# First attention of a two-layer network: the value sums turned by VectorE in 32x32 blocks, with the queries stored in another order

## The chip, the cores and the metric

The kernel runs on one core of a Trainium2 chip, as one program. The metric is the device time of one execution in microseconds (us). Before the change three runs took 5074.21, 5076.88 and 5078.27 us; the median is 5076.88 us.

## The reference

The input is x, 4 batches of 2048 tokens of 256 features, float32. Four blocks follow, each with a layer norm before it, a layer norm after it and a residual sum: a bidirectional scan with decay, a routed mixture with 32 experts, an attention with 16 heads of 16 features and rotary positions, and a sliced attention with 8 heads. The change is in the third:

```python
xq = (x @ wq.T).reshape(B, S, N_HEAD, HEAD_DIM)      # N_HEAD 16, HEAD_DIM 16
xk = (x @ wk.T).reshape(B, S, N_HEAD, HEAD_DIM)
xv = (x @ wv.T).reshape(B, S, N_HEAD, HEAD_DIM)
q = _apply_rope(xq, cos, sin)
k = _apply_rope(xk, cos, sin)
scores = jnp.einsum('bqhd,bkhd->bhqk', q, k) / jnp.sqrt(HEAD_DIM)
attn = jax.nn.softmax(scores, axis=-1)
out = jnp.einsum('bhqk,bkhd->bqhd', attn, xv)
```

B is 4 and S 2048, so there are 64 pairs of batch and head; below each of them is called a head.

## The kernel before

The program is a row of phases, one after the other, with a barrier between them: norm, scan, gate, experts, rope, attention (`at1`), sliced projections, second attention (`at2`), final. Every phase writes each engine's instructions by hand, in order; engines meet only at semaphores. An engine runs its instructions in the order in which they are written, so an instruction that waits holds all behind it.

*The phase before the attention* (`phase_rope`, tag r4) goes through 16 groups of 512 tokens. For each it projects queries, keys and values, turns the pairs, transposes queries and keys to features by tokens (PE into PQ), copies them with ACT into QF (`take_qk`, k = 0 and 1 queries, 2 and 3 keys), and splits them on GpSimd into a rounded part HI and a rest LO, which together hold full float32 for matmuls in the faster float32r. SP stores them with `store_qkv`, two groups behind the projections: the values (`VB`, 1 MB), then HI and LO of the queries (a = 0), then HI and LO of the keys (a = 1). Before its next use VB, HI and LO wait for the semaphore `l_st` of the stores of two groups ago; ACT's `values` is the first to do so. After this on the same queue come the loads of a later group.

*The attention* (`phase_attention` with `TWO` true) makes for each head 64 score tiles of 128 keys by 512 queries, one in each step t of a window of 64 steps. Three things run at once:

- The row maxima, which softmax needs before the exponentials, are computed one head ahead from a second product of queries and keys: PE writes tiles MX (128 queries by 1024 keys, two matmuls) into a ring of two (`RING`), DVE reduces each to a column of NM4 (`maxima`). There are 32 such tiles in a head, one at each even step. At step 50 PE turns the maxima of the next head, ACT copies them (NMF), and GpSimd and SP bring them into two more rows of QT, so that the score matmul subtracts them itself.
- The scores: PE multiplies KT by QT into one of three PSUM slots S (`NSR`), ACT takes the exponential into PB. The score of step t waits for the exponential of step t-3.
- The values: PE multiplies PB by VS, in blocks of 128 keys, each over four steps' tiles, and adds them up in one PSUM buffer AV. VS is 32 columns wide: 16 features, then a column of ones, which gives the softmax's divisor, then zeros. Four chunks of 512 queries stand in AV one below the other, 32 partitions each. A block kb is done in two halves of 256 queries (`PARTS`), the first at step `value_step(kb)` = 4 kb + 6 and the second two steps later. The steps past 63 fall into the next window: block 15 at its steps 2 and 4, and block 0 of the next head at step 6.

*The end of a head*, which the change is about, stands in the next window. At step 4 ACT copies AV into AVS (`put_values`); PE's first AV matmul of the next head waits for that copy. At step 7 (`OUT_STEP`) PE turns AVS with four 128x128 transposes into a slot S (`turn_values`), and ACT copies the slot into FO (`take_values`). At step 11 DVE takes the reciprocals of the divisors, GpSimd multiplies (`normalise_turned`), and SP stores. The transposes take a place in the ring of S, which is why a window has `SITEMS` = 66 places.

```python
PARTS = 2 if TWO else 1
WP = W // PARTS
END_STEP = value_step(NBLK - 1) + 2 * (PARTS - 1)
OUT_STEP = END_STEP + 3 - NSB
```

## Time and profile before

| what | us |
|---|---|
| median of three runs | 5076.88 |
| the profiled execution, its own time | 5076.77 |
| its span, first to last record | 5074.3 |
| PE busy in the span | 4656.5 (92%) |
| DVE busy | 4191.1 (83%) |
| ACT busy | 3425.1 (67%) |
| GpSimd busy | 1333.4 (26%) |

The profile is of one execution, and all shares in it are averages over nine phases with different limits. So a phase is looked at by its stretch of time, given in us from the start of the span. A row of a timeline has the start in us, the length in us, the engine, the line of the kernel, the operation, what it writes and what it reads with the tile's shape (partitions times elements; PE gives rows of the array times columns), how many like it stand in a row, and in brackets how long the engine was idle before and what ended that. Idle time under some 0.1 us is not listed. Two instructions of one engine overlap a little: the next starts before the last has fully ended. PE counts a float32 matmul as two records. PEld is the load of weights, which runs beside PE. A row of stretches has the bounds, the length, the busy time and number of instructions of PE, PEld, DVE, ACT and POOL (GpSimd), then the clock granted to PE (1.00 is 2.4 GHz), the busy share of the DMA engines and what they moved in GB/s.

### The profile page before, as it was taken

What the parts mean: (1) busy time and instruction counts of PE and PEld (TensorE: products, weight loads), DVE (VectorE), ACT (ScalarE), POOL (GpSimd) and SP (SyncE); (2) the same over time, 40 slices, a digit from 0 to 9 for tenths busy, and PEclk for the clock granted to TensorE, in tenths of its full rate; (3) what the DMA queues carried; (4) which work ended last, traced back from release to release, by engine and by line L of the source; (5) the groups of instructions that cost most, each with busy time, mean ns of one, the idle gap of its engine ahead of it and who ended that gap; (6) DMA issues with size and microseconds to landing.
All of it is one profiled execution on the core that took longest, in us unless ns stands there. A gap on an engine that the chain in (4) does not pass through costs nothing. (4 is left out here: it accounts for less than half of the span.)

```text
span 5074.3 us, 90035 instructions
## 1 busy us (share of the span) xinstructions
PE 4656.5 (92%) x33915; PEld 2063.8 (41%) x33915; DVE 4191.1 (83%) x5487; ACT 3425.1 (67%) x6144; POOL 1333.4 (26%) x881
## 2 busy tenths in 40 slices
PE   6998776896999999999999999999998889999993
PEld 3333542562333333333333333333334445555532
DVE  6999640796999999999999999999993877777736
ACT  4878110232888888888888888888885426666663
POOL 2333210462000000000000000000001229999992
PEclk9999887995999999999999999999997769999996
DMA  5111569686333333333333333333313831322305
GB/s 183 58 54 42 187 241 390 201 271 136 49 49 49 49 49 52 53 53 53 49 49 49 49 49 49 54 54 54 49 20 125 297 101 43 82 61 73 79 5 169
DMA packets 383090, 479.51 MB, mean 94 GB/s; under 512 B 164544, under 2 KB 277984, under 8 KB 365760
## 3 DMA queue, kind: packets, MB, share of 16 engines
q1 hardware_dynamic: 369376, 455.41, 38.5%
q10 hardware_dynamic: 13280, 18.35, 1.1%
q8 instruction: 267, 4.37, 0.4%
q14 instruction: 167, 1.37, 0.1%
HBM read 315.71 MB, written 155.58 MB: 93 GB/s over the span
## 5 line engine op out<-in xcount | busy, mean ns | idle before, releaser
L792 DVE TENSOR_REDUCE at_NM<-at_MX 128x1 f32<-128x1024 f32 (+1 forms) x3008 | 3085.7, 1050 | 300.5 <-PE at_MX L614 272.2
L734 ACT ACTIVATE at_PB<-at_S 128x512 f32<-128x512 f32 x5056 | 2720.4, 597 | 587.6 <-PE at_S L643 465.6
L614 PE MATMUL at_MX<-at_KT,at_QT 48*128 48x512 f32 (+1 forms) x5056 | 1920.6, 455 | 58.6 <-DMA at_VS<-v 43.9
L643 PE MATMUL at_S<-at_QT,at_KT 50*128 50x512 f32 (+1 forms) x5056 | 1900.0, 441 | 6.1 <-ACT at_PB L734 5.8
L655 PE MATMUL at_AV<-at_PB,at_VS 128*32 128x256 f32 (+1 forms) x18304 | 1568.6, 414 | 16.6 <-ACT at_AVS L742 15.6
L643 PEld LDWEIGHTS at_S<-at_QT,at_KT 50*128 50x128 f32 (+1 forms) x5056 | 801.6, 187 | 879.0 <-ACT at_PB L734 773.6
L614 PEld LDWEIGHTS at_MX<-at_KT,at_QT 48*128 48x128 f32 (+1 forms) x5056 | 791.2, 190 | 310.2 <-DVE at_NM L792 215.6
L655 PEld LDWEIGHTS at_AV<-at_PB,at_VS 128*32 128x32 f32 x18304 | 363.3, 108 | 859.8 <-ACT at_PB L734 747.5
L548 POOL CAST at_NMR<-at_NMF 16x128 fp32r<-16x128 f32 x79 | 22.1, 279 | 1626.6 <-ACT at_NMF L747 1626.6
L575 POOL TENSOR_TENSOR at_SUM<-at_SUM,at_PB 128x2048 f32<-128x2048 f32 x90 | 415.1, 4612 | 10.9
L935 PE MATMUL wkv_PQ<-wkv_XT,wkv_WT 128*128 128x512 f32 x768 | 341.3, 601 | 50.5 <-DVE wkv_DL L1058 34.1
L575 POOL TENSOR_TENSOR at_SUM<-at_PB 128x2048 f32<-128x2048 f32 x75 | 352.3, 4701 | 30.8 <-ACT at_PB L734 30.1
L558 POOL TENSOR_TENSOR at_O<-at_FO,at_REC 128x256 f32<-128x256 f32 x64 | 39.8, 622 | 1007.4 <-DVE at_REC L803 1007.4
L935 PEld LDWEIGHTS wkv_PQ<-wkv_XT,wkv_WT 128*128 128x128 f32 x768 | 144.9, 192 | 246.3 <-issue 195.0
L1013 POOL TENSOR_TENSOR wkv_EV<-wkv_E2S,wkv_V 128x1024 f32<-128x1024 f32 x32 | 75.5, 2360 | 312.0 <-DVE wkv_MN L1035 132.6
L1223 PE MATMUL r_PA<-r_OC,r_A 128*128 128x256 f32 x512 | 114.8, 383 | 12.5 <-DMA r_A<-ycat 12.5
L1824 PE MATMUL r_QK<-r_WC,r_XT 128*128 128x512 f32 x256 | 120.2, 593 | 0.5 <-DVE r_WC L1983 0.5
L2152 ACT ACTIVATE rows<-moe_PH 128x1024 f32<-128x1024 f32 x8 | 8.2, 1024 | 162.9 <-PE moe_TP L2194 132.1
L1510 PE MATMUL r_PO<-r_XT,r_WS 128*128 128x512 f32 (+2 forms) x136 | 94.9, 861 | 17.8 <-ACT r_XT L1539 17.8
L1223 PEld LDWEIGHTS r_PA<-r_OC,r_A 128*128 128x128 f32 x512 | 97.3, 193 | 27.0 <-DVE r_OC L1331 14.0
L747 ACT ACTIVATE at_NMF<-at_S 16x128 f32<-16x128 f32 x79 | 21.1, 267 | 118.0 <-PE at_S L634 118.0
L2129 DVE COPY rows<-moe_TP 128x128 f32<-128x128 f32 x8 | 2.3, 293 | 115.2 <-PE moe_TP L2194 115.2
(213 smaller groups left out, 3492.6 us busy)
## 6 DMA issues: line engine op xcount, KB each, us to landing
at_QT<-qk SPq DMA_DIRECT2D x402, 128.0 KB, 4.9
moe_W<-in_w SPq DMA_DIRECT2D x48, 1024.0 KB, 11.8
at_KT<-qk SPq DMA_DIRECT2D x384, 128.0 KB, 6.6
qk<-r_HI SPq DMA_DIRECT2D x52, 512.0 KB, 4.7
qk<-r_LO SPq DMA_DIRECT2D x52, 512.0 KB, 5.3
at_VS<-v SPq DMA_DIRECT2D x96, 256.0 KB, 8.7
at_KT<-qk SPq DMA_DIRECT2D x96, 256.0 KB, 6.1
ycat<-wkv_Y SPq DMA_DIRECT2D x32, 512.0 KB, 2.6
```

Of the source, the lines that this page charges most:

```text
L558: nc.gpsimd.tensor_tensor(out, fo[:, :, :, 0:DH], REC[s % 2][:, :, :].to_broadcast([P, W // P, NCH, DH]), ALU.mult).then_inc(norm_done, 1)
L575: nc.gpsimd.tensor_tensor(total[:, :, :], other, PB[:, k:k + NCH, :], ALU.add).then_inc(sum_done, 1)
L614: ins = nc.tensor.matmul(MX[r][:, a, :], q_of(s)[h:h + NQ, b * P:(b + 1) * P], k_of(it, s, b * P // W)[h:h + NQ, (c + a) * W:(c + a + 1) * W],
L643: nc.tensor.matmul(SP_[item(it, s, "score", t)[1]][:, :], k_of(it, s, c)[h:h + NQ + 2, kb * P:(kb + 1) * P], q_of(s)[h:h + NQ + 2, c * W:( ...
L655: ins = nc.tensor.matmul(AV[c * VW:(c + 1) * VW, cols], v_of(it, s, c)[:, kb, :], PB[:, (NCH * kb + c) % NPB, cols], start=first, stop=last)
L734: nc.scalar.activation(PB[:, t % NPB, :], SP_[r][:, :], ACT.Exp, scale=scale).then_inc(exp_done, 1)
L792: nc.vector.tensor_reduce(NM4[:, b, c:c + 1], MX[r][:, :, :].rearrange("p a n -> p (a n)"), AX_X, ALU.max, negate=True).then_inc(ring_got, 1)
L935: ins = nc.tensor.matmul(PQ[q][:, tt * 512:(tt + 1) * 512], WT[:, cc, row:row + P], XT[b % 2][:, cc, t0:t0 + 512], start=(cc == 0), stop=( ...
L1013: nc.gpsimd.tensor_tensor(EV[s][:, :], E2S[s][:, :], V[s][:, :], ALU.mult).then_inc(pv, 1)
L1223: ins = nc.tensor.matmul(PA[u][:, j, :], A[u][:, q, j * P:(j + 1) * P], OC[:, q, :], start=(q == 0), stop=(q == NC - 1))
L1510: ins = nc.tensor.matmul(PO[a][:, h, :], WS[0:k, c, lo:lo + P], XT[u][0:k, c, :], start=(c == 0), stop=(c == len(ks) - 1))
L1824: ins = nc.tensor.matmul(QK[j % 2][:, :], XT[u][:, c, j * P:(j + 1) * P], WC[:, c, 0:2 * D], start=(c == 0), stop=(c == CC - 1))
```

## The change

It has three parts.

1. *The turn.* The copy AVS, the four transposes by PE and the copy FO by ACT are gone for this attention. DVE has one `transpose` of 128x512 from AV in PSUM to FO in SBUF; it turns each block of 32x32 in its place. The block of chunk c and columns 32 j to 32 j + 31 then has 32 queries on partitions 32 c to 32 c + 31 and the 32 columns of the values side by side. It stands at step 2 of the next window, the reciprocal at step 4, the multiply on GpSimd at step 6. The semaphore `avs_ready`, for which PE's next block 0 waits, now comes from DVE.
2. *The last value block.* Both halves of block 15 are done in one step (`part_step`), so that AV is complete at step 2. A window has 65 places in the ring of S.
3. *The order of the queries.* For each partition to hold the queries of its own rows of the output, query 128 b + 32 c + q is now column 512 c + 32 b + q of QT. ACT's copy `take_qk` writes the queries in that order, in runs of 32, and each of HI and LO of the queries is stored with two transfers of 128 partitions by four runs of 128 elements (512 B) in place of one with runs of 512 elements (2 KB). Keys and values are stored as before.

```diff
-    SITEMS = NSB + 1 + TWO
+    SITEMS = NSB + 1
...
-    END_STEP = value_step(NBLK - 1) + 2 * (PARTS - 1)
-    OUT_STEP = END_STEP + 3 - NSB
+    END_STEP = value_step(NBLK - 1)
+
+    def part_step(kb, part):
+
+        return value_step(kb) + (2 * part if kb < NBLK - 1 else 0)
...
             def normalise_turned(it, s):
-                fo = FO[s % 2][:, :].rearrange("p (j c d) -> p j c d", j=W // P, c=NCH)
-                out = O[s % 2][:, :, :].rearrange("p (c j) d -> p j c d", c=NCH)
                 wait(pool, ostored[s % 2], 8 * NSTORE * it - 8 * NSTORE * (s % 2), pool_step)
                 wait(pool, rec_done, it + 1, pool_step)
-                nc.gpsimd.tensor_tensor(out, fo[:, :, :, 0:DH],
-                                        REC[s % 2][:, :, :].to_broadcast([P, W // P, NCH, DH]),
+                nc.gpsimd.tensor_tensor(O[s % 2][:, :, :], FO[s % 2][:, :, 0:DH],
+                                        REC[s % 2][:, :].to_broadcast([P, W // VW, DH]),
                                         ALU.mult).then_inc(norm_done, 1)
...
-            def turn_values(it, s, r):
-
-                wait(pe, avs_ready, it + 1, pe_step)
-                for j in range(W // P):
-                    ins = nc.tensor.transpose(SP_[r][:, j * P:(j + 1) * P], AVS[s % 2][:, j * P:(j + 1) * P],
-                                              ident[:, :])
-                ins.then_inc(s_put, 1)
-
...
-                        if value_step(kb) + 2 * part == t:
+                        if part_step(kb, part) == t:
                             values(n, s, kb, part)
...
-            def take_values(it, s, i, r):
-                wait(act, norm_done, it - 1)
-                wait(act, s_put, i + 1)
-                nc.scalar.activation(FO[s % 2][:, :], SP_[r][:, :], ACT.Copy).then_inc(fo_got, 1)
...
+            def turn_values(it, s):
+
+                wait(dve, norm_done, it - 1)
+                wait(dve, av_done, NBLK * (it + 1))
+                nc.vector.transpose(FO[s % 2][:, :, :].rearrange("p j d -> p (j d)"), AV[:, :]).then_inc(avs_ready, 1)
+
             def invert_turned(it, s):
-                fo = FO[s % 2][:, :].rearrange("p (j c d) -> p j c d", j=W // P, c=NCH)
-                wait(dve, norm_done, it - 1)
-                wait(dve, fo_got, it + 1)
-                nc.vector.reciprocal(REC[s % 2][:, :, :], fo[:, :, :, DH]).then_inc(rec_done, 1)
+                wait(dve, avs_ready, it + 1)
+                nc.vector.reciprocal(REC[s % 2][:, :], FO[s % 2][:, :, DH]).then_inc(rec_done, 1)
...
                         out = qk[a, part].rearrange("(c p) t -> p c t", p=P)
+                        if a == 0:
+                            for c in range(CC):
+                                sp.dma_start(out[:, c, :].rearrange("p (s t) -> p s t", s=E4)[:, :, e * P:(e + 1) * P],
+                                             tile[u][:, c, :].rearrange("p (s t) -> p s t", s=E4).bitcast(F32)).then_inc(l_st[u], 16)
+                            continue
                         sp.dma_start(out[:, :, e * GT:(e + 1) * GT],
                                      tile[u][:, 2 * a:2 * a + 2, :].bitcast(F32)).then_inc(l_st[u], 16)
...
-                nc.scalar.activation(QF[k % 2][:, :], PQ[:, :], ACT.Copy).then_inc(qk_got, 1)
+                out, in_ = QF[k % 2][:, :], PQ[:, :]
+                if k < CC:
+                    out = out.rearrange("p (c j q) -> p j c q", c=E4, j=J)
+                    in_ = in_.rearrange("p (j c q) -> p j c q", c=E4, j=J)
+                nc.scalar.activation(out, in_, ACT.Copy).then_inc(qk_got, 1)
```

How it moves the instructions. First PE at the end of the first head, in the second window, before; each row has the line, the operation, what it writes and reads, and how often. S are scores, MX the tiles of maxima, AV the sums of values.

```order
L614 MATMUL at_MX<-at_KT,at_QT 128x512 x2
L643 MATMUL at_S<-at_QT,at_KT 128x512
L655 MATMUL at_AV<-at_PB,at_VS 32x256 x4
L643 MATMUL at_S<-at_QT,at_KT 128x512
L614 MATMUL at_MX<-at_KT,at_QT 128x512 x2
L643 MATMUL at_S<-at_QT,at_KT 128x512
L655 MATMUL at_AV<-at_PB,at_VS 32x256 x4
L674 MATMUL at_S<-at_ident,at_AVS 128x128 x4
L643 MATMUL at_S<-at_QT,at_KT 128x512
L614 MATMUL at_MX<-at_KT,at_QT 128x512 x2
L643 MATMUL at_S<-at_QT,at_KT 128x512
```

and with the change:

```order
L638 MATMUL at_S<-at_QT,at_KT 128x512
L650 MATMUL at_AV<-at_PB,at_VS 32x256 x8
L638 MATMUL at_S<-at_QT,at_KT 128x512
L611 MATMUL at_MX<-at_KT,at_QT 128x512 x2
L638 MATMUL at_S<-at_QT,at_KT 128x512 x2
L611 MATMUL at_MX<-at_KT,at_QT 128x512 x2
L638 MATMUL at_S<-at_QT,at_KT 128x512
L650 MATMUL at_AV<-at_PB,at_VS 32x256 x4
```

The four transposes between the last AV of one head and the next scores are gone; the four AV matmuls of the last half have joined the four before them (x8), and the two scores after the next MX pair stand with no AV between them.

Next DVE, over the same window, from the end of the maxima's preparation on, before (L792 are the tiles of maxima, L797 the last step of a head's maxima):

```order
L797 TENSOR_REDUCE at_NM<-at_NM 128x16
L792 TENSOR_REDUCE at_NM<-at_MX 128x1 x17
L803 RECIPROCAL at_REC<-at_FO 128x16
L792 TENSOR_REDUCE at_NM<-at_MX 128x1 x15
L797 TENSOR_REDUCE at_NM<-at_NM 128x16
```

and with the change:

```order
L768 TENSOR_REDUCE at_NM<-at_NM 128x16
L763 TENSOR_REDUCE at_NM<-at_MX 128x1 x13
L774 STREAM_TRANSPOSE at_FO<-at_AV 128x512
L763 TENSOR_REDUCE at_NM<-at_MX 128x1
L778 RECIPROCAL at_REC<-at_FO 128x16
L763 TENSOR_REDUCE at_NM<-at_MX 128x1 x18
L768 TENSOR_REDUCE at_NM<-at_NM 128x16
```

The transpose stands one tile of maxima before the reciprocal, and the reciprocal three tiles earlier than before.

Last SP in the phase before the attention, the stores of one group and the loads behind them, before:

```order
L1709 DMA x<-r_X 128x1024
L1716 DMA v<-r_VB 128x16x128
L1722 DMA qk<-r_HI 128x2x512
L1722 DMA qk<-r_LO 128x2x512
L1722 DMA qk<-r_HI 128x2x512
L1722 DMA qk<-r_LO 128x2x512
L1701 DMA r_A<-routed 32x512
```

and with the change:

```order
L1687 DMA x<-r_X 128x1024
L1694 DMA v<-r_VB 128x16x128
L1702 DMA qk<-r_HI 512x1x128 x2
L1702 DMA qk<-r_LO 512x1x128 x2
L1705 DMA qk<-r_HI 128x2x512
L1705 DMA qk<-r_LO 128x2x512
L1679 DMA r_A<-routed 32x512
```

HI and LO of the queries are two transfers each (x2), of 512 runs of 128 elements; nothing else moves.

## Rows read from the trace of the kernel before

**Rows 1.** Stretches: the phase before the attention, and the attention.

```profile
903.70:1172.00 268.30, 249.47 (x1032) 162.17 (x1032) 223.94 (x532) 79.15 (x160) 161.99 (x198) 0.96 0.78 259
1172.00:3862.00 2690.00, 2637.75 (x24896) 995.51 (x24896) 2513.05 (x2180) 2293.08 (x4289) 93.39 (x196) 0.98 0.36 49
```

**Rows 2.** The same view, of 2500 us in the middle of the attention.

```profile
1290.00:3790.00 2500.00, 2484.85 (x23819) 938.12 (x23819) 2400.27 (x2083) 2193.86 (x4104) 82.78 (x184) 1.00 0.36 50
```

**Rows 3.** Timeline of DVE over one head of the attention.

```profile
1419.92 0.24 DVE L803 RECIPROCAL at_REC<-at_FO 128x16 f32<-128x16 f32 x1
1420.09 18.54 DVE L792 TENSOR_REDUCE at_NM<-at_MX 128x1 f32<-128x1024 f32 x15
1438.66 0.19 DVE L797 TENSOR_REDUCE at_NM<-at_NM 128x16 f32<-128x32 f32 x1
...
1458.36 2.45 DVE L792 TENSOR_REDUCE at_NM<-at_MX 128x1 f32<-128x1024 f32 x2 [0.90 <-PE at_MX L614]
1460.72 0.25 DVE L803 RECIPROCAL at_REC<-at_FO 128x16 f32<-128x16 f32 x1
```

**Rows 4.** Timeline of PE at the end of the same head.

```profile
1413.76 0.40 PE L643 MATMUL at_S<-at_QT,at_KT 50*128 50x512 f32 x1
...
1414.09 0.64 PE L655 MATMUL at_AV<-at_PB,at_VS 128*32 128x256 f32 x8
...
1414.66 0.50 PE L643 MATMUL at_S<-at_QT,at_KT 50*128 50x512 f32 x1
...
1415.00 0.40 PE L643 MATMUL at_S<-at_QT,at_KT 50*128 50x512 f32 x1
...
1415.64 0.64 PE L655 MATMUL at_AV<-at_PB,at_VS 128*32 128x256 f32 x8 [0.24 <-ACT at_AVS L742]
...
1416.21 0.66 PE L674 MATMUL at_S<-at_ident,at_AVS 128*128 128x128 f32 x4
...
1416.79 0.49 PE L643 MATMUL at_S<-at_QT,at_KT 50*128 50x512 f32 x1
```

**Rows 5.** Timelines: DVE ahead of the first scores, ACT and PE in the last head.

```profile
1227.37 17.06 DVE L792 TENSOR_REDUCE at_NM<-at_MX 128x1 f32<-128x1024 f32 x15 [1.36 <-PE at_MX L614]
...
3845.09 11.80 ACT L734 ACTIVATE at_PB<-at_S 128x512 f32<-128x512 f32 x21
...
3856.95 1.07 PE L655 MATMUL at_AV<-at_PB,at_VS 128*32 128x256 f32 x16 [0.18 <-ACT at_PB L734]
```

**Rows 6.** Groups of DVE instructions by line: busy us, mean ns of one.

```profile
L1066 DVE TENSOR_TENSOR_SCAN wkv_DEN<-wkv_E1S,wkv_DEN,wkv_E2S 128x1024 f32<-128x1024 f32 x32 | 77.2, 2411 | 0.0
...
L809 DVE TENSOR_TENSOR at_O<-at_L,at_AVS 128x512 f32<-128x512 f32 x15 | 10.2, 682 | 78.9 <-ACT at_L L760 78.9
```

**Rows 7.** Phase before the attention: two stretches, then timelines of ACT and PE.

```profile
1008.00:1010.00 2.00, 2.00 (x15) 1.65 (x13) 1.93 (x4) 0.82 (x3) 1.92 (x3) 1.00 1.05 290
1012.00:1014.00 2.00, 2.00 (x8) 1.07 (x8) 1.77 (x8) 0.60 (x1) 0.28 (x2) 1.00 1.04 383
...
1003.65 0.84 ACT L1898 ACTIVATE r_VB<-r_PV,r_RS 128x256 f32<-128x256 f32 x2 [3.74 <-DMA qk<-r_LO]
...
1018.16 0.84 ACT L1898 ACTIVATE r_VB<-r_PV,r_RS 128x256 f32<-128x256 f32 x2 [2.85 <-PE r_PV L1834]
...
1005.03 0.66 PE L1844 MATMUL r_PQ<-r_ident,r_QR 128*128 128x128 f32 x4
...
1020.11 0.60 PE L1844 MATMUL r_PQ<-r_ident,r_QR 128*128 128x128 f32 x4
```

**Rows 8.** What ended ACT's idle time before L1898: us in all, times.

```profile
  PE r_PV L1834: 85.6, 28
  DMA qk<-r_LO: 13.8, 4
```

**Rows 9.** Timeline at the end of the attention, ACT's copy and DVE's reciprocal.

```profile
3858.08 0.60 ACT L742 ACTIVATE at_AVS<-at_AV 128x512 f32<-128x512 f32 x1 [1.19 <-PE at_AV L655]
...
3860.25 0.25 DVE L803 RECIPROCAL at_REC<-at_FO 128x16 f32<-128x16 f32 x1 [34.81 <-ACT at_FO L752]
```

More of the change, by code:

```diff
@@ L336, in places @@
         for t in range(NSB):
-            if TWO and t == OUT_STEP and (not isinstance(n, int) or n > 0):
-                out.append(("out", 0))
             out.append(("score", t))
@@ L347, in item @@
         if not isinstance(n, int):
-            return SITEMS * n - TWO + 1 + k, (SITEMS * s - TWO + 1 + k) % NSR
-        i = SITEMS * n - (TWO if n else 0) + 1 + k
+            return SITEMS * n + 1 + k, (SITEMS * s + 1 + k) % NSR
+        i = SITEMS * n + 1 + k
         return i, i % NSR
@@ L368, in phase_attention @@
         PB = m.sb("PB", [P, NPB, W])
-        AVS = [m.sb(f"AVS{u}", [P, W]) for u in range(2)]
         NM4 = m.sb("NM4", [P, NBLK, NMX // NBLK])
@@ L376, in phase_attention @@
             O = [m.sb(f"O{u}", [P, NBLK, DH]) for u in range(2)]
-            REC = [m.sb(f"REC{u}", [P, W // P, NCH]) for u in range(2)]
-            FO = [m.sb(f"FO{u}", [P, W]) for u in range(2)]
+            REC = [m.sb(f"REC{u}", [P, W // VW]) for u in range(2)]
+            FO = [m.sb(f"FO{u}", [P, W // VW, VW]) for u in range(2)]
         else:
+            AVS = [m.sb(f"AVS{u}", [P, W]) for u in range(2)]
             ONES = m.sb("ONES", [P, VW])
@@ L588, in window @@
                         adds(*unit)
-                    if TWO and t == OUT_STEP + 4 and (not isinstance(n, int) or n > 0):
+                    if TWO and t == END_STEP + 4 - NSB and (not isinstance(n, int) or n > 0):
                         normalise_turned(n - 1, s + NBUF - 1)
@@ L626, in slot_free @@
                     wait(pe, exp_done, NSB * of + x + 1, pe_step)
-                elif kind == "turn":
+                else:
                     wait(pe, nmf_got, of + 2, pe_step)
-                else:
-                    wait(pe, fo_got, of, pe_step)
             def max_turn(it, r):
@@ L697, in window @@
                     tile = tile_at(t)
-                    if TWO and t == OUT_STEP and (not isinstance(n, int) or n > 0):
-                        slot_free(n, "out")
-                        turn_values(n - 1, s + NBUF - 1, item(n, s, "out")[1])
                     if tile and later(n, tile[0]):
@@ L737, in put_values @@
             def put_values(it, s):
-                if not TWO:
-                    wait(act, norm_done, it - 1)
+                wait(act, norm_done, it - 1)
                 wait(act, av_done, NBLK * (it + 1))
@@ L763, in window @@
                 for t in range(NSB):
-                    if TWO and t == OUT_STEP and (not isinstance(n, int) or n > 0):
-                        take_values(n - 1, s + NBUF - 1, *item(n, s, "out"))
                     exps(n, s, t)
                     for it, s_, t_ in running(n, s, t):
-                        if END_STEP == t_:
+                        if not TWO and END_STEP == t_:
                             put_values(it, s_)
@@ L777, in _ @@
             rounds(act, window)
-            put_values(N - 1, N - 1)
-            if TWO:
-                take_values(N - 1, N - 1, TAIL, TAIL % NSR)
-            else:
+            if not TWO:
+                put_values(N - 1, N - 1)
                 put_sums(N - 1)
@@ L830, in window @@
                             outputs(*unit)
-                    if TWO and t == OUT_STEP + 4 and (not isinstance(n, int) or n > 0):
+                    if TWO and t == END_STEP - NSB and (not isinstance(n, int) or n > 0):
+                        turn_values(n - 1, s + NBUF - 1)
+                    if TWO and t == END_STEP + 2 - NSB and (not isinstance(n, int) or n > 0):
                         invert_turned(n - 1, s + NBUF - 1)
@@ L834, in _ @@
             if TWO:
+                turn_values(N - 1, N - 1)
                 invert_turned(N - 1, N - 1)
@@ L1741, in _ @@
             for u in range(2):
[L1742 removed]
+                sp.wait_ge(l_st[u], 56 * NGR)
         @block.gpsimd
@@ L1773, in split @@
                 if k == 0:
-                    wait(pool, l_st[u], 80 * (g // 2))
+                    wait(pool, l_st[u], 112 * (g // 2))
                 wait(pool, qk_got, 4 * g + k + 1)
@@ L1894, in values @@
                 wait(act, rs1, g + 1)
-                wait(act, l_st[u], 80 * (g // 2))
+                wait(act, l_st[u], 112 * (g // 2))
                 for jj in range(2):
```

8 lines of the change are left out of this document (1 added, 7 removed).

## The prediction

> **What bounds the kernel now.** I read the profile from the outside in. The table of stretches first: the first attention takes 2690 us of the span, the stage before it (the one that writes its queries) 268 us [rows 1]. The change touches only these two. In 2500 us of the attention's middle PE is busy 2484.9 us, or 99.4%, DVE 96%, ACT 88%, at a granted clock of 1.00 [rows 2]. That PE is busy is not yet that it binds, so the next view is DVE's row of work in time: each head of 64 steps repeats after 1460.72 - 1419.92 = 40.80 us [rows 3]. Fifteen tiles of maxima take 18.57 us there (1420.09 to 1438.66), 1.238 us each, in which PE does a pair of steps. Where PE had nothing else to do, DVE took fifteen in 17.06 us, 1.137 each; where DVE had nothing to do, ACT took 21 exps in 11.80 us, 1.124 for two [rows 5]. So DVE has 0.10 us to spare in each 1.24 and ACT 0.11, and **PE sets the pace**.
>
> Then PE's timeline over one head's end [rows 4]. A pair of scores, with an MX pair beside it, starts at 1414.66 and the next at 1416.79, 2.13 apart where 1.24 is usual: 0.89 us is lost. The reader sees both parts: the AV matmuls at 1415.64 waited for ACT's copy of AV (after the score before them they would have begun 0.33 later, as 1413.76 and 1414.09 show; that score began at 1415.00, so 0.31 is lost), and four transposes hold PE from 1416.21 to the next score at 1416.79, 0.58. Together 0.89. DVE's idle 0.90 before its tile of 1458.36 [rows 3] is the same loss seen from behind. The rest of the 40.80 is 32 x 1.238 = 39.6 and about 0.3 at the turn of the maxima, which stays.
>
> **The change, part by part.**
>
> *PE and ACT at a head's end.* Four transposes, the copy into AVS and the copy into FO go, and with them the wait of AV for AVS: 0.89 us of PE per head in 63 of 64 heads. ACT's two copies (0.60 each) were off the bound, they only caused the wait.
>
> *The last value block.* Its second half moves from two steps later into the same step. PE's order has eight AV matmuls in one place and none in the next. The profile counts each as two records: eight records hold PE 0.57 (1414.09 to 1414.66), sixteen last 1.07 against 0.64 [rows 4, 5], so the double block holds 1.00. Call its start 0. From the rows, the second score of a pair starts 0.34 after the first (1414.66, 1415.00) and what follows 0.33 later. So the next scores start at 1.00, 1.34 and 1.67, the one after at 2.01, and that one needs the slot whose exp comes from the score of 1.00: done 0.49 later [rows 4], exp of 0.56 [rows 5], and by my estimate 0.1 of signals, 2.15. PE stands 0.14 us there, and the AV block after it starts at 2.34 + 0.14 = 2.48, which is where two pairs of 1.24 would put it. So what the merged block saves (1.00 for twice 0.57) the wait takes back, and the sum is 0; ACT catches up with its 0.11 per pair.
>
> *DVE's transpose.* The trace before has no such instruction. Below it lies the cheapest row with 512 columns from PSUM, 0.68 us (the multiply of the second attention); above it the scan, 2.41 for 1024, so 1.21 for 512 [rows 6]. I take 0.70, since it reads each column once as the multiply does; DVE starts its next instruction 0.07 before the end of the last (the reciprocal lasts 0.24 from 1419.92, the next starts at 1420.09 [rows 3]), so it takes 0.63 of DVE. Where does it stand? Tile 2's matmuls end at 0.05, so DVE works on it until 1.2; the AV block ends at 1.07, so the transpose does not wait. It holds DVE until 1.8, tile 4 until 2.95 (done, and its slot free, at 3.05), the reciprocal adds 0.17 (1419.92 to 1420.09), tile 6 until 4.25 (free at 4.35). PE needs those two slots at 3.05 and 4.29. So DVE's extra work just about fits in the slack of the ring of two tiles; with a signal's 0.06 I allow 0.12 us for it per head. Queued behind the transpose on DVE is tile 4, and PE's tile 8 waits for that. PE's first AV matmul of the next head (at 2.48) waits for the transpose, done at 1.9: covered by 0.6.
>
> The Trainium skill (VectorE: DVE Perf Modes, The three transpose paths) gives 311 ns for 128x128 bf16 on DVE against 390 ns on TensorE. No run here shows it; four such blocks would make 1.24 us, an estimate from that page, and by that the head would gain 0.23 and the time be 5066 us, as in the first rival. Against it stand the reciprocal of 16 columns at 0.24 us [rows 3] and 512 columns at 0.68 [rows 6]: some 0.23 of any DVE instruction is fixed, and four times 0.31 would count that four times.
>
> *Gain per head:* 0.89 - 0.12 = 0.77, with the bounds 0.89 (nothing stands) and 0.26 (a transpose of 1.21 costs 0.51 more). 63 x 0.77 = 48.5 us.
>
> *The last head.* From the end of AV to the reciprocal: 3858.08 to 3860.25, 2.17 us [rows 9]. Now one transpose, 0.65: saves 1.5 us. GpSimd's multiply reads another layout of the same size and stays.
>
> *The stage before: queries stored in another order.* ACT copies with the same 512 columns, runs of 32: I take it as 0.60 still, and ACT is 70% idle there. The stores of HI and LO for the queries go from 2 transfers of 2 KB packets to 4 of 512 B, 32 more issues on SP, 2 in each of 16 groups. In front of them stands nothing new; behind them on SP are the key stores and the loads of a later group, which have a group's time in hand. In a stretch with 512 B packets (the values') the DMA engines move 290 GB/s, in one with 2 KB packets 383, both full [rows 7]. So 1.05 MB takes 3.62 us in place of 2.74: +0.88 us per group. The Trainium skill (DMA: Bandwidth & Descriptors, Specifications) has 512 B as the least size for line rate; the trace disagrees by that quarter, and its number decides (by the page the term would be 0). Is it hidden? A group takes 15.08 us (PE's transposes at 1005.03 and 1020.11), DMA is busy 78% on average [rows 1], so throughput is there. But ACT's scaling of the values waits for the landing of the stores of two groups ago: in 4 of 32 cases DMA released it [rows 8]. At 1003.65 it did [rows 7], 0.57 us after the place that the next group's (1018.16 - 15.08) gives. After it comes ACT's QF copy, 0.6 us as any of 512 columns, and PE waits for that: 1018.16 + 0.84 + 0.60 = 1019.6 against 1020.11, 0.5 us to spare, and none in the group before [rows 7]. So a landing 0.88 later passes on up to 0.88 to PE in a group like the first and little in others, and a late PE gives the next group's stores more time. I take 0.25 us x 14 groups = 3.5, and 0.9 for the last stores, after which the attention may begin: +4.4 us. Bounds: 0, and 14 x 0.88 + 1.8 = 14 us.
>
> **Sum.** Against the profiled execution's own 5076.77 us (span 5074.3, 2.5 around it; the median of the three runs is 5076.88, the same): -48.5 - 1.5 + 4.4 = -45.6, so 5031 us.
>
> **The rivals.**
> 1. *DVE becomes the bound.* The transpose costs what a scan costs, 1.21 us. DVE has little slack: 0.10 per tile. Tile 4 comes 0.51 later, PE stands for its slot, and the head gains 0.77 - 0.51 = 0.26. 63 x 0.26 = 16.4, the last head saves 1.0 and the stores cost 4.4: 5064 us. For it: DVE is at 96%. Against it: a scan carries each result into the next, a transpose does not; the multiply's 0.68 is the nearer row [rows 6].
> 2. *The query stores bind the stage before.* All of the 0.88 in every group and 1.8 at its end, +14 instead of +4.4: 5040 us. For it: the landing already is on the edge. Against: 28 of 32 waits end with PE.
> 3. *Slower: PE waits for the transpose.* AV has one buffer. If the 32x32 turn of 4-byte data takes 1.9 us, over half again the scan's pace, everything behind it on DVE comes 1.2 later than in my sum: the head loses 0.12 + 1.2 against 0.89 gained, +0.43 x 63 = 27, with the stores 5108 us. It decides from about 1.47 us of transpose on, where 0.77 is used up. For it: nothing of the kind is in the trace. Against it: even the scan is at 1.21.
> 4. *The change does nothing*, because what looks like PE's loss is a wait that comes back elsewhere (in ACT's exps): 5075 to 5082 us. Against it: ACT's pace alone is 1.12 [rows 5].
>
> **How the numbers follow.** Forecast 0.72, rival 1 0.11, rival 2 0.09, rival 3 0.05, rival 4 0.03. The predicted time is the forecast's 5031. Its own ends are 5019 (all 0.89 gained, 56.1, 1.5 for the last head, the stores free) and 5050 (0.50 per head, 31.5, with the 1.5, and the stores at 6); rival 2 lies inside. To leave out no more than 2 in 10, the range goes from 5019 to 5058, most of the way to rival 1. A change of under 0.2%, 10 us, cannot be told from none: faster 0.88 (rival 1, at 13 us, counts mostly here), the same 0.07, slower 0.05.
>
> **What would show it.** In the profile after: the row of the transpose, 0.65 to 0.75 us, 64 of them; the head's period from reciprocal to reciprocal 40.0 us; pairs of scores around the double AV block 1.67 and 0.67 apart and the pair after them at its usual place; DVE's idle time from MX at the head's end nearly gone, and PE waits for DVE's maxima that were not there before, about 0.1 us each; the stage before at 15.1 to 15.4 us per group with more of ACT's waits ended by LO's stores; the attention's stretch 2640 us. It is wrong if the period stays over 40.5 (rival 1 or 4: the transpose's duration tells which), or if the stage before grows by over 10 us.

## The result

The change takes 5029.51 us (median of 4 runs, 5026.30 to 5031.53), the kernel before on the same chip 5075.56 (4 runs). The ratio is 0.9904, 95% interval 0.9890 to 0.9918: faster by about 1%. Predicted was 5031, from 5019 to 5058. The profiled execution took 5029.49 us, its span 5027.3, 47.0 less than before.

| | before | after |
|---|---|---|
| span, us | 5074.3 | 5027.3 |
| PE busy | 4656.5 (92%) | 4622.3 (92%) |
| DVE busy | 4191.1 (83%) | 4207.0 (84%) |
| ACT busy | 3425.1 (67%) | 3361.4 (67%) |
| head's period, reciprocal to reciprocal, mean of 61 | 40.83 | 40.10 |
| first store of x to first load of KT | 261.01 | 265.79 |
| first load of KT to last reciprocal | 2681.54 | 2633.82 |

The last two lines are read from the timelines of SP's queue and of DVE: 915.23, 1181.02 and 3814.84 after, 917.70, 1178.71 and 3860.25 before. The attention gives 47.7 us, the stage before it takes 4.8, what lies behind the attention is 1.6 shorter and what lies ahead of both 2.5, though the change touches neither; together 47.0.

The groups of the page that answer to the change (the line, engine, operation, tiles, count, busy time, mean ns, idle time before and what ended it), in the changed kernel:

```profile
L763 DVE TENSOR_REDUCE at_NM<-at_MX 128x1 f32<-128x1024 f32 (+1 forms) x3008 | 3066.3, 1049 | 241.1 <-PE at_MX L611 216.2
...
L715 ACT ACTIVATE at_PB<-at_S 128x512 f32<-128x512 f32 x5056 | 2712.1, 597 | 628.3 <-PE at_S L638 503.7
...
L555 POOL TENSOR_TENSOR at_O<-at_FO,at_REC 128x256 f32<-128x256 f32 x64 | 39.9, 624 | 749.8 <-DVE at_REC L778 749.8
```

The stretches, as [rows 1, 2] before; the columns are the same:

```profile
903.70:1172.00 268.30, 251.65 (x1032) 161.90 (x1032) 223.60 (x532) 79.06 (x160) 158.96 (x195) 0.96 0.82 254
...
1290.00:3700.00 2410.00, 2407.83 (x23146) 917.88 (x23139) 2370.48 (x2104) 2093.57 (x3907) 81.00 (x180) 1.00 0.38 51
```

PE was busy 99.4% of the middle; now it is 99.9%. In the page's groups DVE's wait for MX is 216 us in the whole program, where it was 272. ACT waits for scores 504 us for 466 before, in which time it has fewer copies to make; it is off the path. GpSimd's multiply lasts 0.62 us as before.

DVE over one head, as [rows 3]:

```profile
1413.77 0.71 DVE L774 STREAM_TRANSPOSE at_FO<-at_AV 128x512 f32<-128x512 f32 x1
1414.40 1.19 DVE L763 TENSOR_REDUCE at_NM<-at_MX 128x1 f32<-128x1024 f32 x1
1415.51 0.23 DVE L778 RECIPROCAL at_REC<-at_FO 128x16 f32<-128x16 f32 x1
1415.67 21.93 DVE L763 TENSOR_REDUCE at_NM<-at_MX 128x1 f32<-128x1024 f32 x18
1437.64 0.19 DVE L768 TENSOR_REDUCE at_NM<-at_NM 128x16 f32<-128x32 f32 x1
1437.86 5.96 DVE L763 TENSOR_REDUCE at_NM<-at_MX 128x1 f32<-128x1024 f32 x5
1444.03 9.94 DVE L763 TENSOR_REDUCE at_NM<-at_MX 128x1 f32<-128x1024 f32 x8 [0.22 <-PE at_MX L611]
1453.89 0.71 DVE L774 STREAM_TRANSPOSE at_FO<-at_AV 128x512 f32<-128x512 f32 x1
...
1455.63 0.23 DVE L778 RECIPROCAL at_REC<-at_FO 128x16 f32<-128x16 f32 x1
```

The turn of the values lasts 0.71 us, in all 64 heads between 705 and 718 ns. The idle 0.90 of [rows 3] is gone; 0.22 at the turn of the maxima stays. PE's timeline at the same head's end, as [rows 4], and ACT's:

```profile
1411.86 0.50 PE L638 MATMUL at_S<-at_QT,at_KT 50*128 50x512 f32 x1
...
1412.53 1.07 PE L650 MATMUL at_AV<-at_PB,at_VS 128*32 128x256 f32 x16
1413.53 0.50 PE L638 MATMUL at_S<-at_QT,at_KT 50*128 50x512 f32 x1
...
1413.87 0.39 PE L638 MATMUL at_S<-at_QT,at_KT 50*128 50x512 f32 x1
...
1414.11 0.40 PE L638 MATMUL at_S<-at_QT,at_KT 50*128 50x512 f32 x1
...
1414.78 0.50 PE L638 MATMUL at_S<-at_QT,at_KT 50*128 50x512 f32 x1
1415.21 0.64 PE L650 MATMUL at_AV<-at_PB,at_VS 128*32 128x256 f32 x8
1415.78 0.50 PE L638 MATMUL at_S<-at_QT,at_KT 50*128 50x512 f32 x1
```

```profile
1414.13 2.06 ACT L715 ACTIVATE at_PB<-at_S 128x512 f32<-128x512 f32 x4 [0.59 <-PE at_S L638]
```

From the pair at 1411.86 to the pair at 1415.78 it is 3.92 us, where three pairs take 3.72: PE still loses 0.20 per head. It does so ahead of the score of 1414.78. That one needs the slot of the score of 1413.53, whose exp starts at 1414.13, 0.10 after the score's end, and is done some 0.56 later, at 1414.69. No row of PE names a tile of maxima as what it waits for: between 1300 and 3800 us the view of the MX matmuls lists no wait for DVE, where it lists 62 with the turn done twice (run 3). PE stands for ACT's exp, which runs 2 and 4 bear out.

### The profile page after: what moved, and what is told of

Same layout as the page of the kernel before. It is cut to its first block and busy times, and to the rows that moved or that the text cites. A ratio compares the mean times of both kernels' runs of the same rounds, so it can differ in the third digit from the quotient of the medians.

```text
span 5027.3 us, 89365 instructions
## 1 busy us (share of the span) xinstructions
PE 4622.3 (92%) x33659; PEld 2057.7 (41%) x33659; DVE 4207.0 (84%) x5551; ACT 3361.4 (67%) x6016; POOL 1333.6 (27%) x881
## 5 line engine op out<-in xcount | busy, mean ns | idle before, releaser
L1885 ACT ACTIVATE r_VB<-r_PV,r_RS 128x256 f32<-128x256 f32 x64 | 26.8, 470 | 108.4 <-PE r_PV L1817 65.7
```

## The experiments

Totals of one kernel scatter by up to 21 us between executions, on one chip too (ten of run 1 lie between 5061.70 and 5082.63). So what decides below is the period of a head and the stretches of the profile; the ratio stands beside them. A period below is the time between two reciprocals, given with both; the mean of 61 heads of the same profile differs from it by 0.02 us at most, except in run 6, where both are given.

**1. The last block not merged.** Its second half back at two steps later, the turn at step 4.

```diff
-    END_STEP = value_step(NBLK - 1)
+    END_STEP = value_step(NBLK - 1) + 2 * (PARTS - 1)
-        return value_step(kb) + (2 * part if kb < NBLK - 1 else 0)
+        return value_step(kb) + 2 * part
```

> The change with its second part undone: the second half of block 15 stands at step 4 again, DVE's transpose after tile 4, the reciprocal at step 6. Theory A: the merged block is what lets DVE turn ahead of tile 4. Without it the transpose starts when tile 4 is reduced, 2.47 us after the first half's start, and is done at 3.17, while PE wants AV for the next head at 2.48: PE waits 0.75 us per head in place of the 0.20 that the change still loses. 63 x 0.55 = +35: 5064 us, period of a head 40.65. Theory B: the 0.20 that is left comes from the merged block (the score after it is late, and an exp with it), and the transpose fits anywhere: -0.20 x 63 = -13: 5017 us, period 39.9.

Measured: period 1336.99 - 1296.31 = 40.68; 5069.87 us, ratio 0.9988 (0.9978 to 0.9998). PE at the head's end:

```profile
1334.94 0.40 PE L638 MATMUL at_S<-at_QT,at_KT 50*128 50x512 f32 x1
1336.01 0.64 PE L650 MATMUL at_AV<-at_PB,at_VS 128*32 128x256 f32 x8 [0.68 <-DVE at_FO L774]
```

The AV block would have started at 1335.27; it stands 0.74 until DVE's transpose is done. The transposes and ACT's copies are gone here too, and yet only 0.15 of the 0.89 is won. Merging the last block, which the prediction booked at 0, is what lets the turn run beside PE's work: it is worth 0.58 of the 0.73. The period came as theory A had it (40.65).

**2. A turn of 32 columns.** It leaves out 15 of 16 parts of the turn (the rest of FO holds ones), so that most of the attention's output is missing.

```diff
-                nc.vector.transpose(FO[s % 2][:, :, :].rearrange("p j d -> p (j d)"), AV[:, :])...
+                nc.vector.transpose(FO[s % 2][:, 0, :], AV[:, 0:VW])...
```

> The change with only 32 of the 512 columns of AV turned (the other columns of FO hold ones, so most of the attention's output is left out). DVE's instruction shrinks from 0.71 to about 0.2 us. Theory A: DVE's turn is hidden, the 0.20 us left per head are PE waiting for the exp behind the merged block: same time as the change, 5029 us within 3, period 40.1. Theory B: the 0.20 are the ring of two tiles, held by DVE: period 39.9, 5017 us.

Measured: period 1349.09 - 1308.97 = 40.12, 5031.05 us, ratio 0.9911 (0.9894 to 0.9928).

```profile
1307.30 0.20 DVE L774 STREAM_TRANSPOSE at_FO<-at_AV 128x32 f32<-128x32 f32 x1
1307.83 1.23 DVE L763 TENSOR_REDUCE at_NM<-at_MX 128x1 f32<-128x1024 f32 x1 [0.33 <-PE at_MX L611]
```

DVE gets 0.51 us back, waits 0.33 for PE before the next tile, and the period is the change's. So in the changed kernel the turn is free, and the 0.20 left is not DVE's.

**3. A second turn, elsewhere and in the same place.** Once in the middle of the window, where nothing depends on it:

```diff
+                    if TWO and t == 20 and n > 0:
+                        nc.vector.transpose(SCR[:, :], FO[(n - 1) % 2][:, :, :].rearrange("p j d -> p (j d)"))
```

> The change with one more transpose of 128x512 on DVE at step 20 of each window, from FO in SBUF to a tile that nobody reads. It adds 0.63 us of DVE per head at a place where DVE has nothing else to catch up with. Theory A (PE binds, DVE has 0.10 us of slack per tile and 0.5 us of lead in the ring): PE waits 0.05 to 0.15 us per head, 5032 to 5039 us. Theory B (DVE at 98% binds): all of it shows, 63 x 0.63 = 40: 5069 us.

and once right ahead of the turn that is there, from AV into a scratch tile:

```diff
+                nc.vector.transpose(SCR[:, :], AV[:, :])
```

> The change with the turn done twice at the same place, first into a tile that nobody reads, then into FO. 0.63 us more of DVE per head, as in the run with the transpose in mid-window (which cost 0.05 us per head), but ahead of tile 4. Theory A (after the merged block there is no lead left: tile 4 is reduced by 3.05 now and PE writes into its slot at 3.25): tile 4 is done at 3.7, PE waits 0.45 us for its slot, period 40.12 + 0.45 = 40.57, 63 x 0.45 = 28 more than the change: 5058 us. Theory B (the ring of two has 0.5 us of lead at every place): +0.05 again, 40.17, 5033 us.

Measured in the middle: period 1342.91 - 1302.75 = 40.16, 0.06 more than 40.10 (5038.18 us, ratio 0.9919, 0.9900 to 0.9937). At the head's end: 1342.97 - 1302.38 = 40.59, 0.49 more (5065.06 us, ratio 0.9973, 0.9957 to 0.9989). PE there, with the turn doubled:

```profile
1342.06 0.64 PE L651 MATMUL at_AV<-at_PB,at_VS 128*32 128x256 f32 x8
1342.63 0.50 PE L639 MATMUL at_S<-at_QT,at_KT 50*128 50x512 f32 x1
1343.10 0.50 PE L612 MATMUL at_MX<-at_KT,at_QT 48*128 48x512 f32 x2
```

and DVE:

```profile
1341.27 0.67 DVE L776 STREAM_TRANSPOSE at_FO<-at_AV 128x512 f32<-128x512 f32 x1
1341.86 1.19 DVE L764 TENSOR_REDUCE at_NM<-at_MX 128x1 f32<-128x1024 f32 x1
```

An MX pair starts with the score beside it, at 1342.63, elsewhere; here it is 0.47 later, because tile 4's maxima (1341.86, 1.19 long) end at 1343.05. DVE came to tile 4 0.59 later (1341.27 to 1341.86, the second turn less the overlap), so 0.10 of that is hidden and 0.49 is paid, through the ring's slot. That gives rival 3 its number: a turn of 0.71 + 0.10 + 0.73 = 1.54 us would use up the gain of a head, an estimate from these rows, where the prediction had 1.47.

**4. The score ahead of the double block.** Can the 0.20 be had? The score of step 3 goes ahead of the merged block, so that its exp is not the late one.

```diff
-                    scores(n, s, t)
+                    if not (TWO and t == 3 and n > 0):
+                        scores(n, s, t)
+                    if TWO and t == 2 and n > 0:
+                        scores(n, s, 3)
```

> The change with PE's score of step 3 placed ahead of the merged block of AV matmuls instead of behind it. ACT gets its exp in time, and the 0.2 us for which the score of step 6 waits for that exp should go. But AV is complete 0.33 us later, so DVE's transpose, tile 4 and its slot come about 0.2 to 0.3 us later. Theory A (the next wait, for tile 4's slot, takes its place at once): period 40.1, 5024 to 5032 us. Theory B (the exp is the only thing that stands): period 39.8 to 39.9, 5010 to 5016 us.

Measured: period 3738.79 - 3698.59 = 40.20, 0.10 worse; 5043.0 us, ratio 0.9926 (0.9907 to 0.9946). DVE and PE at another head's end:

```profile
1364.46 0.72 DVE L777 STREAM_TRANSPOSE at_FO<-at_AV 128x512 f32<-128x512 f32 x1
1365.10 1.19 DVE L766 TENSOR_REDUCE at_NM<-at_MX 128x1 f32<-128x1024 f32 x1
```

```profile
1365.94 0.50 PE L638 MATMUL at_S<-at_QT,at_KT 50*128 50x512 f32 x1
1366.34 0.51 PE L611 MATMUL at_MX<-at_KT,at_QT 48*128 48x512 f32 x2
```

The wait for the exp is gone. But the double block now stands behind one score more: DVE turns AV 2.13 after the start of the pair ahead of it (1362.33 in this trace), where in the change it was 1413.77 - 1411.86 = 1.91. Tile 4 is read until 1366.29, and the MX pair starts 0.40 after the score that it usually starts with. The next wait took the place of the one removed, and it is longer: theory A's mechanism, at 0.10 more than its 40.1. The run does not show what that wait would be with AV complete as early as in the change.

**5. The second half one step later.**

```diff
-        return value_step(kb) + (2 * part if kb < NBLK - 1 else 0)
+        return value_step(kb) + (2 * part if kb < NBLK - 1 else part)
```

> The change with the second half of block 15 one step later (step 3, behind that step's score) instead of in the same step. The score of step 3 is late by nothing, so no exp is late. AV is complete at 1.55 instead of 1.07 after the block's start. Theory A (two lanes bind at the end of a head, the exp's and the tile slot's): the transpose ends at 2.2, tile 4 at 3.4, PE wants its slot at 3.05 and waits 0.4 in place of the 0.2 for the exp: period 40.3, 5042 us. Theory B (only the late exp costs): period 39.9, 5017 us.

Measured: period 3723.12 - 3682.61 = 40.51, 0.41 worse; 5055.63 us, ratio 0.9956 (0.9942 to 0.9971). DVE:

```profile
1330.84 0.72 DVE L774 STREAM_TRANSPOSE at_FO<-at_AV 128x512 f32<-128x512 f32 x1 [0.37 <-PE at_AV L650]
```

Both expectations miss. DVE reaches the turn before AV is complete and stands 0.37, and tile 4 behind it (until 1331.48 + 1.18 = 1332.66) and PE's slot with it:

```profile
1332.41 0.50 PE L638 MATMUL at_S<-at_QT,at_KT 50*128 50x512 f32 x1
1332.72 0.51 PE L611 MATMUL at_MX<-at_KT,at_QT 48*128 48x512 f32 x2
```

That is theory A's wait; the head loses 0.21 more than A said (40.3), of which no run tells the parts. In the changed kernel DVE arrives just after AV is complete: 1413.77 against an end of 1412.53 + 1.07 = 1413.60. Three other orders of the head's end have now been tried (runs 1, 4 and 5), and the change's own is the best of them.

**6. The transposes alone.** The 0.89 of [rows 4] was split by reading into 0.58 for PE's transposes and 0.31 for ACT's copy. Here ACT copies AV to FO at step 4 as before, the last block is not merged, as in run 1, and DVE's turn is out: there is no turn by anyone, nor the division (the reciprocal reads ones). Of the edit, the copy and the reciprocal:

```diff
+                dst = FO[s % 2][:, :, :].rearrange("p j d -> p (j d)") if TWO else AVS[s % 2][:, :]
-                nc.scalar.activation(AVS[s % 2][:, :], AV[:, :], ACT.Copy).then_inc(avs_ready, 1)
+                nc.scalar.activation(dst, AV[:, :], ACT.Copy).then_inc(avs_ready, 1)
...
-                nc.vector.reciprocal(REC[s % 2][:, :], FO[s % 2][:, :, DH]).then_inc(rec_done, 1)
+                nc.vector.reciprocal(REC[s % 2][:, :], CST[:, :, DH]).then_inc(rec_done, 1)
```

> The change without DVE's turn: ScalarE copies the value sums from PSUM to FO at step 4, at the place where the kernel before copied them to AVS; no transposes by PE, no second copy, the second half of block 15 at step 4 as before. Left out: the turn of the values, and the division by the sums (the reciprocal reads a tile of ones). It splits the 0.89 us that PE lost per head before, 40.83 us per head, into the transposes and the wait for the copy. Theory A, the sum as predicted: the four transposes were lost in full, 0.58, and the wait for ScalarE's copy stays, 0.24 to 0.31, so a period of 40.2 to 40.3; PE's row of values of the next head still waits 0.2 to 0.3 for at_FO by ACT. Theory B: the place that the transposes took was partly cover for the copies and for DVE, so that taking them away gives less than 0.4: 40.45 or more. Theory C: with the transposes gone ScalarE's copy is no longer waited for either: 39.95 to 40.1, better than the change.

Measured: period 1342.50 - 1302.22 = 40.28 for the first, and 40.23 as the mean of 61, which goes against the 40.83 before; 5039.45 us, ratio 0.9922 (0.9904 to 0.9940).

```profile
1300.65 0.40 PE L639 MATMUL at_S<-at_QT,at_KT 50*128 50x512 f32 x1
1301.29 0.64 PE L651 MATMUL at_AV<-at_PB,at_VS 128*32 128x256 f32 x8 [0.24 <-ACT at_FO L724]
```

The transposes, with ACT's second copy, cost 40.83 - 40.23 = 0.60, and the wait stays, 1301.29 - 1300.98 = 0.31: the split was right, theory A.

**7. The stage before the attention.** Three kernels, and then the change and the last of the three once more. First the old order of the query stores, with ACT's copy plain again (the attention then reads its queries in the old order, and its rows come out in another):

```diff
-                        if a == 0:
-                            for c in range(CC):
-                                sp.dma_start(... [:, :, e * P:(e + 1) * P], ...)
-                            continue
...
-                out, in_ = QF[k % 2][:, :], PQ[:, :]
-                if k < CC:
-                    out = out.rearrange("p (c j q) -> p j c q", c=E4, j=J)
-                    in_ = in_.rearrange("p (j c q) -> p j c q", c=E4, j=J)
-                nc.scalar.activation(out, in_, ACT.Copy).then_inc(qk_got, 1)
+                nc.scalar.activation(QF[k % 2][:, :], PQ[:, :], ACT.Copy).then_inc(qk_got, 1)
```

> The change with its third part undone: ACT copies the queries in token order and they are stored in 2 KB runs (so the attention's rows come out in a wrong order). Theory A: 512 B packets cost the phase before the attention what its stretch grew by, 4.8 us (first store to the attention's first load, 261.0 to 265.8): 5025 us, that stretch 261. Theory B: the growth is scatter between executions: 5029 us and a stretch near 266 or anywhere between.

Then the new number of transfers with the old pieces of 2 KB (a group's queries in four transfers, where before there were two):

```diff
-                                sp.dma_start(out[:, c, :].rearrange("p (s t) -> p s t", s=E4)[:, :, e * P:(e + 1) * P],
-                                             tile[u][:, c, :].rearrange("p (s t) -> p s t", s=E4).bitcast(F32))...
+                                sp.dma_start(out[:, c, e * GT:(e + 1) * GT],
+                                             tile[u][:, c, :].bitcast(F32))...
```

> The change, with the query stores still cut into one transfer per plane of 128 rows, but each of them with the old addresses: 128 rows of 2 KB in a piece where the change has pieces of 512 bytes. ScalarE still permutes. The rows of the queries end up in the wrong order. It tells the size of the pieces from the number of the transfers. Theory A (the pieces of 512 bytes make the stores slow): the stretch from the first store of x to the first load of KT, 261.01 us before, 265.79 with the change and 260.54 with the old stores, comes back to 261.0, at most 262. Theory B (four transfers in place of one, issued and completed one after the other, make them late): it stays at 265 to 266. Period of a head in attention 40.1 by both.

Then the change with a semaphore of their own for the values' stores, so that ACT's scaling of the values waits for these alone and not for the later stores of HI and LO:

```diff
+        v_st = [m.sem(f"v_st{u}") for u in range(2)]
-                sp.dma_start(out[:, :, e * J:(e + 1) * J, :], VB[u][:, :, :, :]).then_inc(l_st[u], 16)
+                sp.dma_start(out[:, :, e * J:(e + 1) * J, :], VB[u][:, :, :, :]).then_inc(v_st[u], 16)
...
-                wait(act, l_st[u], 112 * (g // 2))
+                wait(act, v_st[u], 16 * (g // 2))
```

> The change with a semaphore of its own for the stores of the values, so that ACT's scaling waits for the values' store alone and not for the queries' and keys'. GpSimd's split still waits for those. Theory A (the new stores cost time through this wait, which ended 11 of ACT's waits before L1885 after the change and 4 before it): the stretch from the first store of x to the attention's first load falls from 265.8 to 261.5 to 262.5, only the last stores stay longer; 5026 us. Theory B (512 B packets make the DMA engines the bound of that phase): stretch 265 to 266, 5029 us.

And the change and this kernel again, on one chip:

> The change once more, unchanged, timed on the same chip as the run after it, since totals of other chips cannot be set against each other below 0.2%. Period of a head 40.10 and rope stretch 265.8 again, attention from the first load of KT to the last reciprocal 2633.8. If single profiles scatter by more than 1 us in the rope stretch, the price of the stores is less sure than the difference of two profiles makes it look.

> The values' own semaphore once more, beside the change on the same chip. Theory A (the stores' delay reaches the end only through ScalarE's wait for buffers, and nothing later takes it up): the rope stretch is 261 to 262 as before, attention 2634 to 2636, and the median is 4 us less than that of the change, some 0.08%. Theory B (what the rope phase gains is lost behind it): stretch 261 to 262, median within 1 us of the change's.

The stretch, cut by the stores of x, of which there is one per group (from the timeline of SP's queue, in us):

| kernel | 1st to 2nd | 2nd to 16th, 14 groups | 16th to first load of KT | sum | ACT's waits ended by DMA | median, ratio (interval) |
|---|---|---|---|---|---|---|
| before | 12.01 | 210.84 | 38.16 | 261.01 | 4, 13.8 us | |
| the change | 12.01 | 214.56 | 39.22 | 265.79 | 11, 42.6 | above |
| the change again | 12.00 | 214.65 | 39.15 | 265.80 | 11, 42.6 | 5031.87, 0.9905 (0.9889 to 0.9922) |
| runs 1 to 6 (same stage) | 12.0 or 13.5 | 211.64 to 215.01 | 39.15 to 39.22 | 262.82 to 267.66 | 11 to 14, 42.7 to 49.4 | |
| old stores | 12.00 | 210.39 | 38.15 | 260.54 | 5, 17.0 | 5026.01, 0.9900 (0.9885 to 0.9916) |
| four transfers of 2 KB pieces | 12.01 | 213.07 | 38.18 | 263.26 | 12, 43.6 | 5031.54, 0.9910 (0.9895 to 0.9925) |
| own semaphore | 12.01 | 210.00 | 39.27 | 261.28 | none | 5034.74, 0.9916 (0.9901 to 0.9931) |
| own semaphore again | 13.37 | 210.00 | 39.29 | 262.66 | none | 5029.43, 0.9902 (0.9887 to 0.9916) |

Three things are seen. The third column of the stretch is 38.15 to 38.18 in the three kernels with pieces of 2 KB and 39.15 to 39.29 in all those with pieces of 512 bytes: **the size of the pieces costs 1.0 us at the end**, whatever the number of transfers. The 14 groups take 210.00, 15.0 each, as soon as ACT no longer waits for the stores of HI and LO: **all the rest is that wait**. And the wait goes with the number of transfers: four of 2 KB pieces have as much of it as the change (12 times, 43.6 us), two of 2 KB pieces little (4 and 5 times), here with four and then with two (the view of r_VB on ACT, what ended its idle time):

```profile
  DMA qk<-r_LO: 43.6, 12
```

```profile
  DMA qk<-r_LO: 17.0, 5
```

From the issue of a group's first query store to the landing of its last store, the median of the 3rd to 14th group is 11.77 and 11.55 us with two transfers, 12.80 with four of 2 KB pieces and 12.84 in the change; in the 16th group it is 7.98, 7.98, 8.00 and 8.73. So in the middle it is the number that makes the stores late, and at the end the pieces. As a time, the middle of the four transfers is 2.2 to 2.7 us above the kernels with two. In the kernels whose stage is the change's it varies between 211.6 and 215.0, so the 213.07 lies inside, and no run shows that the pieces add anything there. The sum, 263.26, met neither expectation (261 to 262, 265 to 266), since each of the two causes has its own place.

The wait in the lines of ACT, in this stage; in the change, then with the semaphore of their own:

```profile
L1885 ACT ACTIVATE r_VB<-r_PV,r_RS 128x256 f32<-128x256 f32 x64 | 26.8, 470 | 108.4 <-PE r_PV L1817 65.7 <-DMA qk<-r_LO 42.6
```

```profile
L1887 ACT ACTIVATE r_VB<-r_PV,r_RS 128x256 f32<-128x256 f32 x64 | 26.8, 470 | 97.1 <-PE r_PV L1819 97.1
```

DMA ended 11 of these waits with the change, 4 before [rows 8], none with the own semaphore.

Is that kernel faster than the change? By the stretch by 3.1 to 4.5 us; the medians on one chip, 5029.43 and 5031.87, differ by 2.4 in the expected sense, where single runs of each spread over 12 and 14 us. The first time its median was 5034.74, where 5026 was expected. As a total it is unclear: neither theory of the last expectation (4 us, within 1 us) is shown. The attention of the change took 2640.53 us this time, where 2633.8 was expected; the last section shows why.

## Why the prediction held

*PE sets the pace.* It does: a second turn in the middle of a window costs 0.06 of 0.63, and a turn of 0.20 us gains nothing.

*0.89 lost per head, 0.31 and 0.58.* Shown by run 6: 0.31 and 0.60.

*The merged block, "the sum is 0".* The times within it came as worked out, scores at 1.00 and 1.34 after its start. The third came at 1.58 for 1.67, the one that waits at 2.25 for 2.15, since ACT's exp began 0.10 after the score ended and the prediction counted this 0.1 on one side only. The AV block behind it came at 2.68 for 2.48: after standing, the score took 0.43 to the next block where 0.33 is usual. So PE stands 0.20 longer than the merging saves. What this step missed is what the merging is for: without it (run 1) the turn ends in PE's way, and 0.58 of the gain goes.

*DVE's turn, 0.70, and 0.12 for the ring.* The turn is 0.71. The 0.12 was booked for the ring's slot of tile 4, and in the change nothing waits for it: the slot is free at 3.06 after the double block's start (1414.40 + 1.19), as worked out (3.05), but PE, held by the exp, asks for it at 3.25. The reason was wrong, and the size near, because a wait of much the same length stood in front. Run 2, with a turn of a third of the length and the same period, shows that DVE's part was nothing. In run 4 the front wait is gone, and one for the ring stands there, with the turn 0.22 later. This is the step of the sum that failed: 0.12 for DVE should have been 0.20 for the exp, with DVE's hidden behind it. Among the signs named beforehand, PE's waits for DVE's maxima, about 0.1 us each, did not come.

The Trainium skill (VectorE: DVE Perf Modes, The three transpose paths), with four times its 311 ns for 128 columns of bf16, would have made 1.24 us; the traces have 0.706 for 512 columns of float32 and 0.206 for 32, so 0.50 us for 480 more, 1.04 ns each, and 0.17 that come once. By these two, 128 columns would take 0.31 us, an estimate that agrees with the skill's figure: what was too long was to count the once four times, as the prediction said.

*Gain per head 0.77.* Measured 0.73; 63 x 0.73 = 46.0 for 48.5. By the starts of the exps, as the median over the heads, 0.91 was lost at a head's end before and 0.20 is now, and 0.02 more is won at the turn of the maxima. *The last head, 1.5.* From the start of its last AV block to the reciprocal it is 3.30 before (3856.95 to 3860.25) and 1.96 now (3812.88 to 3814.84): 1.3. Together 47.3 of the measured 47.7; the rest lies in the first head, where the clock rises (last section).

*The query stores, +4.4.* Measured +4.8. The end came as worked out, 1.0 for 0.9 (0.88 a group by [rows 7]), from the size of the pieces. The middle is 3.7 for 3.5, and the path was right, ACT's wait for the stores of two groups ago, which run 7 takes away; the cause was not. The prediction had the stores land later because small pieces move more slowly; run 7 shows the same waits, and landings as late, with pieces of 2 KB in four transfers, and the prediction gave the larger number of transfers no price. In other executions the middle was 0.8 to 4.2 above before. So that 3.7 is near 3.5 is luck. The Trainium skill's 512 bytes as enough for line rate (DMA: Bandwidth & Descriptors, Specifications) would have made this term 0; the 1.0 us at the end goes against it here.

*The rivals.* 1 (DVE binds) fell with the 0.71 of the turn; 2 (+14) with the +4.8; 3 needed a turn of 1.5 us; 4 (nothing) with the period. Rival 3's mechanism is real all the same: runs 1 and 3 show both forms of it, PE waiting for the turn and PE waiting for the tile behind it.

*The total.* In the profiled executions it is -47.7 + 4.8 = -42.9 for -45.6 forecast, and 4.1 us more from stretches that the change does not touch made the span 47.0 shorter. The medians, 46.05 apart, cannot be split up like this. With totals that scatter by more than 5 us, that the median came within 2 us of the forecast is in part luck; that it lies in the range is not.

## What to carry to other kernels

Moving a short operation from a pacing engine to a nearly full one can pay, if it starts just after its input is complete and ends before anyone asks: here the same 0.71 us was free in one place, cost 0.06 in another, and took back 0.58 of 0.73 where, with the last block not merged, it stood two steps later. Behind a wait that a timeline shows can stand another of almost its length: two orders that took the exp's wait away (runs 4 and 5) brought one for the tile's slot that was longer. And a buffer's release is better counted by a semaphore of its own: a shared count made the values wait for stores that had nothing to do with them, 3.1 to 4.5 us in that stage, though the total does not show it clearly.

## What was not expected of the hardware

Much of the scatter of the totals has a place. The attention begins at half the clock, and the moment at which it rises differs between executions. The same three stretches of two executions of the change (the profile above, and "the change again"; the clock is the third number from the end):

```profile
1240.00:1260.00 20.00, 19.33 (x99) 7.24 (x97) 14.12 (x13) 10.37 (x19) 0.00 (x0) 0.50 0.35 47
1260.00:1280.00 20.00, 20.00 (x172) 7.11 (x168) 16.62 (x16) 14.61 (x27) 0.00 (x0) 0.84 0.00 1
1280.00:1300.00 20.00, 19.96 (x196) 7.95 (x193) 19.62 (x19) 17.22 (x34) 1.35 (x3) 1.00 0.29 43
```

```profile
1240.00:1260.00 20.00, 19.32 (x99) 7.25 (x97) 14.11 (x13) 10.37 (x19) 0.00 (x0) 0.50 0.36 48
1260.00:1280.00 20.00, 20.00 (x114) 6.72 (x112) 11.48 (x10) 9.81 (x18) 0.00 (x0) 0.50 0.00 1
1280.00:1300.00 20.00, 20.00 (x181) 7.27 (x183) 17.54 (x16) 15.84 (x30) 0.72 (x2) 0.91 0.01 3
```

After gaps of 0.34 us, the last at 1242, PE is busy almost without one, and still at 1.2 GHz, with pairs of scores 2.16 apart for 1.24; the step to 2.4 GHz comes at about 1266 in the first and 1284 in the second. From the first load of KT to the first reciprocal it is 114.20 and 121.71 us; over all kernels here that turn by DVE it was 107.91 to 123.99. Of the 10.2 us between these two executions of the change, 7.5 lie in this stretch and 3.6 behind the attention. This one moment is worth up to 16 us, a third of what the whole change brings, and it is why parts of a change were judged here by periods and not by totals. What sets the moment is not shown by any run.
